# A decoder in one kernel: norm's root ahead of weight splits, embeddings transposed ahead of the bias, a tile's softmax sums transposed behind its own probabilities

## The reference

```python
x = x + recurrent(layernorm(x))                 # conv, gates, a linear scan, GELU gate, output product
x = x + aft(layernorm(x) + ctx, pos_bias, ...)  # keys, values, exp(pos_bias) band, two layernorms, an MLP
for l in range(2):                              # attention over windows of 128 tokens, then an MLP
    q, k, v = split(shift(x) @ wqkv[l]); q, k = rotary(l2norm(q) * qs), rotary(l2norm(k) * ks)
    p = exp(q @ k.T + mask)                     # 8 heads of 64; a tile of 128 queries sees two tiles of keys
    x = x + ((p @ v) / p.sum(-1)) @ wo[l]
    x = x + mlp(layernorm(shift(x)))
```

## Time and profile before

| | |
|---|---|
| time, median of 3 runs | 1028.35 us (1028.14 to 1028.93) |
| the profiled execution: time, span | 1023.85 us, 1022.0 us |
| busy: PE, DVE | 949.0 us (93%), 664.5 us (65%) |
| busy: ACT, POOL | 511.1 us (50%), 414.3 us (41%) |
| mean TensorE clock granted | 0.987 of full speed |

### The profile page before, as it was taken

One profiled execution on the slowest core, in us unless ns is written; L12 is line 12 of the kernel. 1 busy time (PEld: TensorE's weight loads), 2 busy tenths in 40 slices (PEclk: granted clock), 3 DMA queues, 4 the chain that ended last, 5 costly groups with the idle time before them and its releaser, 6 DMA issues.

```text
span 1022.0 us, 17391 instructions
## 1 busy us (share of the span) xinstructions
PE 949.0 (93%) x5656; PEld 766.2 (75%) x5656; DVE 664.5 (65%) x1686; ACT 511.1 (50%) x1217; POOL 414.3 (41%) x416
## 2 busy tenths in 40 slices
PE   5889969999999997999999889999999999979998
PEld 4668855767676875888888777888787878768887
DVE  6879576357574577667666545667766676745653
ACT  4577731403122234666666664444766666664443
POOL 4333523112012247766767410004766666621110
PEclk9899979999999998999999999999999999999999
DMA  6202013000000000000000020000000000100101
GB/s 248 73 1 62 21 42 108 1 0 1 0 0 1 1 22 0 2 23 0 21 0 28 16 93 23 4 4 23 1 2 22 0 21 0 35 15 17 32 24 45
DMA packets 15236, 26.32 MB, mean 26 GB/s; under 512 B 1162, under 2 KB 11776, under 8 KB 14416
## 3 DMA queue, kind: packets, MB, share of 16 engines
q1 hardware_dynamic: 15184, 25.68, 7.7%
HBM read 20.53 MB, written 2.10 MB: 22 GB/s over the span
## 4 chain that ended last, share of the span: by engine, by line
PE 74%; DVE 9%; ACT 6%; issue 4%; POOL 4%; SPq 2%; DMA 1%; DVEq 0%; ACTq 0%; POOLq 0%
PE bank L1540 31%; PE bank L1874 6%; PE bank L1687 5%; PE bank L1829 5%; PE bank L1735 5%; PE bank L1839 4%; PE bank L1853 4%; ACT probs L1406 2%; PE bank L1816 2%; PE bank L1864 2%; SPq L342 1%; PE bank L1698 1%; PE bank L1947 1%; PE bank L1808 1%; POOL scanned L410 1%
## 5 line engine op out<-in xcount | busy, mean ns | idle before, releaser
L1406 ACT ACTIVATE probs<-bank,row_min 128x256 f32<-128x256 f32 (+1 forms) x256 | 111.6, 463 | 122.6 <-DVE row_min L998 122.6
L542 POOL TENSOR_TENSOR norms<-norms,minus_half 128x16 f32<-128x16 f32 x32 | 93.6, 2924 | 2.7
L998 DVE CUSTOM_DVE_ANT_0 bank<-bank,mask 128x256 f32<-128x256 f32 (+1 forms) x256 | 90.8, 429 | 5.7 <-PE bank L1829 5.6
L1540 PE MATMUL bank<-wqkv_hi,x_hi 128*128 128x512 f32 x192 | 82.5, 430 | 1.8 <-DVE rot L974 1.1
L1540 PE MATMUL bank<-wqkv_lo,x_hi 128*128 128x512 f32 x192 | 76.3, 398 | 0.0
L1540 PE MATMUL bank<-wqkv_hi,x_lo 128*128 128x512 f32 x192 | 75.9, 395 | 0.0
L1135 DVE SCALAR_TENSOR_TENSOR hidden<-bank,lcols,hidden 128x512 f32<-128x512 f32 (+1 forms) x48 | 36.0, 750 | 50.9 <-PE bank L1540 28.2
L1839 PE MATMUL bank<-ident,probs 128*128 128x128 f32 x448 | 61.5, 279 | 3.7 <-ACT probs L1406 3.7
L524 POOL TENSOR_TENSOR q_tok<-rot 128x512 f32<-128x512 f32 x32 | 41.3, 1290 | 57.7 <-DVE rot L974 57.7
L1540 PE MATMUL bank<-t_hi,wm_hi 128*128 128x512 f32 x160 | 63.6, 397 | 0.0
L1540 PE MATMUL bank<-t_lo,wm_hi 128*128 128x512 f32 x160 | 63.5, 397 | 0.0
(11 more groups left out here) (240 smaller groups left out, 2642.5 us busy)
## 6 DMA issues: line engine op xcount, KB each, us to landing
w_stage<-in_wm_l_dram SPq DMA_DIRECT2D x8, 534.0 KB, 3.7
w_stage<-in_wqkv_dram SPq DMA_DIRECT2D x2, 1536.0 KB, 7.9
out_dram<-stream SPq DMA_DIRECT2D x8, 256.0 KB, 2.4
emb<-in_ctx_dram SPq DMA_DIRECT2D x1, 1536.0 KB, 6.7
inner<-in_w_gate_dram SPq DMA_DIRECT2D x1, 1152.0 KB, 10.1
stream<-in_x_dram SPq DMA_DIRECT2D x2, 512.0 KB, 5.6
stream<-in_x_dram SPq DMA_DIRECT2D x1, 1024.0 KB, 12.5
ew<-in_pos_bias_dram SPq DMA_DIRECT2D x1, 1024.0 KB, 11.3
```

The source lines that it names most:

```text
L542: pool.tensor_tensor(norms[:, 2, :], norms[:, 1, :], minus_half[:, :], ALU.pow).then_inc(c_rn, 1)
L998: dve.tensor_tensor_reduce(logits, logits, mask[:, 2 * P - nk:2 * P], 1.0, FAR, ALU.add, ALU.min, row_min[:, w % 2, 2 * i + e:2 * i + e + ...
L1406: act.activation(probs[:, i, e, 0:nk], logits, ACT.Exp, bias=row_min[:, w % 2, h:h + 1], scale=-1.0, accum_out=row_sum[:, w % 2, h:h + 1]) ...
L1540: ins = pe.matmul(out, stationary, moving, start=(first and i == 0), stop=(last and i == len(terms) - 1))
```

## The change

Four places change; no computation is added or removed.

1. First stage: POOL splits the first of the three gate weight pieces ahead of `rstd_of(1)` and not behind it; DVE makes `m4sp` between the statistics of batch 1 and their use; ACT makes `gelu_gate(0)` ahead of `transposed_out(1)`.
2. Second stage: `rstd_of(NB)` stands ahead of the seven weight splits on POOL.
3. `transpose_emb(0)` stands ahead of `bias_by_key(0)` on PE, and its copies in the same place on ACT.
4. Attention: `transpose_sums(n)` stands in window n, behind the last transpose of its probabilities, and writes bank 3; ACT's copy stands behind the copy of the last transposed probabilities. `weigh_values` waits for that copy, since it writes bank 3 next, and `transpose_k` for the residual of n - 2.

```diff
@@ POOL
             rstd_of(0)
-            rstd_of(1)
-
             pool.wait_ge(wg_in, 16)
             for k in range(KR):
+                if k == 1:
+                    rstd_of(1)
...
+            rstd_of(NB)
             pool.wait_ge(wx_in, 64)
...
             pool.wait_ge(aft_in, 48)
-            rstd_of(NB)
             keep_emb(0)
@@ DVE
             dve.wait_ge(a_tp, 2)
-            norm(1, 1)
+            norm_stats(1, 1)
             dve.wait_ge(col_in, 16)
-            conv_taps(0, 0)
-            conv_taps(0, 1)
-            low_part(1, a_tp_out, a_tp_lo)
-            conv_low(0, 0)
-            conv_taps(0, 2)
-            conv_low(0, 1)
             dve.tensor_scalar(fb_tmp[:, 2, :], cols[:, C_FB:C_FB + KR], 0.0, None, ALU.max).then_inc(fb_vec, 1)
...
             dve.tensor_scalar(m4sp[:, :], fb_tmp[:, 2, :], -4.0, None, ALU.mult).then_inc(fb_vec, 1)
+            norm_apply(1, 1, False)
+            conv_taps(0, 0)
+            conv_taps(0, 1)
+            low_part(1, a_tp_out, a_tp_lo)
+            conv_low(0, 0)
+            conv_taps(0, 2)
+            conv_low(0, 1)
             conv_low(0, 2)
@@ ACT
             taps(0)
+            gelu_gate(0)
             transposed_out(1)
-            gelu_gate(0)
...
+            transposed_emb(0)
             bias_transposed(0)
             bias_transposed(1)
-            transposed_emb(0)
...
                 act.wait_ge(c_ot_out, n)
-                act.activation(rsum_t[:, :], bank[2][:, :], ACT.Copy).then_inc(c_rt_out, 1)
+                act.activation(rsum_t[:, :], bank[3][:, :], ACT.Copy).then_inc(c_rt_out, 1)
...
                 exps(n, w, 1)
-                if prev:
-                    sums_transposed(n - 1)
...
                 probs_transposed(n, w, KI - 1)
+                sums_transposed(n)
                 if two:
                     values(n + 2, (w + 2) % TT)
...
-                sums_transposed(n0 + NT - 1)
@@ PE
+            transpose_emb(0)
             bias_by_key(0)
             bias_by_key(1)
-            transpose_emb(0)
...
                 pe.wait_ge(c_v, n + 1)
-                pe.wait_ge(c_ot_out, n)
+                pe.wait_ge(c_rt_out, n + 1)
...
                 pe.wait_ge(c_rb, n + 1)
-                if not (isinstance(n, int) and n == 0):
-                    pe.wait_ge(c_res, n)
+                pe.wait_ge(c_ot_out, n)
                 for i in range(KI):
-                    ins = pe.transpose(bank[2][:, i * P:(i + 1) * P],
+                    ins = pe.transpose(bank[3][:, i * P:(i + 1) * P],
...
                 if keyed:
                     pe.wait_ge(c_qt, n + 3)
+                else:
+                    pe.wait_ge(c_res, n)
...
                 score_pairs(n, w)
                 if prev:
-                    transpose_sums(n - 1)
                     weigh_values(n - 1, (w - 1) % TT)
...
-                    transpose_k(n + 1, (w + 1) % 2, [(c_rt_out, n)] if prev else [])
+                    transpose_k(n + 1, (w + 1) % 2, [(c_res, n - 1)] if prev else [])
...
                 transpose_probs(n, w, KI - 1)
+                transpose_sums(n)
                 if two:
                     qkv(n + 2, (w + 2) % TT, 2)
...
-                transpose_sums(n0 + NT - 1)
                 weigh_values(n0 + NT - 1, TT - 1)
```

## The result

| | before | changed |
|---|---|---|
| time, median | 1028.24 us (1027.26 to 1028.93, 4 runs) | 1012.3 us (1011.3 to 1013.42, 4 runs) |
| the profiled execution: time, span | 1023.85, 1022.0 us | 1013.18, 1011.4 us |
| its mean granted TensorE clock | 0.987 | 0.985 |

The ratio is 0.9845, with a 95% interval of 0.9823 to 0.9868: 15.9 us faster.

What follows compares the result with a forecast made beforehand. PE, busy 93% of the span, bounds the kernel, with holes where it waits for DVE. Terms 9.5 + 0.8 + 5.2 = 15.5 us off 1023.85 give 1008.35, plus 4.5 to the median: 1012.9 us, range 1007.5 to 1018.5.

Steps and rivals of the forecast that it cites:

- The second stage: Root ahead of POOL's weight splits, embeddings' transposes ahead of the bias: `project` starts 9.5 us earlier.
- The sign of error that I had named: Forecast is wrong if PE idles ahead of the sums' transposes or `project` waits for POOL's low parts beyond 135.
- The rival of strict turns: POOL and DVE alternate strictly: second stage gives 7.9 us, 11.7 us in all, 1016.7 us; chance 0.2.
- The first stage: Root of batch 1 1.0 us later, taps 1.9 us shorter: PE starts 0.8 us earlier.
- The attention: Sums' transposes moved behind the probabilities: 2.6 us off a layer, 5.2 us for two.
- The ordinary window: PE-bound attention windows, n = 2 to 12 without w = 1: 0.18 us off each, 1.6 us in nine.
- the new change from scores to weighing: PE's shape change in attention windows: bounds nothing to 0.37 us, taken as 0.19.
- n = 14: Attention tile waiting on DVE's keys: 1.0 us of idling goes, less 0.5 for the sums, 0.5 us off.
- The last tile: End of an attention layer: ACT's copies end earlier, output product at 599.25 instead of 600.06, 0.8 us off.
- The sums' wait: Rival: PE waits for the sums in each of some 26 attention windows, 1031 us at 0.7 us each; chance 0.04.
- The gain of the second stage: Rival had it given back, the residual waiting for something else: only 6.0 us left, 1022.4 us; chance 0.04.
- the free change: Rival: attention's new shape change free, clock up at the bias, DVE held little: 19.7 us off, 1008.7 us; chance 0.17.

Runs made afterwards that it cites:

- the first experiment: The changed kernel timed once more without any edit (also called the repeat): 1010.92 us, 0.9837 of the kernel before.
- early splits and a later `keep_emb(0)`: Changed kernel with the ten weight splits moved to where POOL idles and `keep_emb(0)` behind DVE's low part of the embeddings: 1008.61 us.
- the root put back: Changed kernel with POOL making the first stage's root of batch 1 ahead of all gate splits again: 1013.93 us.
- last experiment: Changed kernel with the weighing of tile n - 1 behind two thirds of the product of n + 2 on PE: 1049.13 us.
- the attention's part alone: Kernel before with only the change's attention hunks: 1021.62 us, ratio 0.9938.
- the three groups: Experiments timed beside the kernel before, each group sharing a chip; medians of before 1027.98, 1027.63 and 1029.88 us.

## Why the prediction held, and where it didn't

The time was in the range, 0.6 us from the forecast. By its steps:

**The second stage.** Forecast 9.5 us, measured 10.05 to `project`; the low clock in the profiled execution then took back 1.5 us of it there, and in the execution of the first experiment nothing. DVE's pieces came as placed: `normed` 2.57 (2.4), the gated inputs 3.81 (3.9), the wait 1.41. My bias at half its slow time (0.97) measured 1.06; of the 10.05 us, 0.9 are the bias at the full clock. What I had under-estimated is how the splits suffer: 10.3 us instead of 7.8. The low parts that `project` waits for ended at 135.47, as late as DVE's own (135.49) and PE's bias (135.50). My "at 130.8 if nothing holds them" left out that they are held, and by luck this cost nothing. The sign of error that I had named, `project` waiting for low parts beyond 135, came by the letter; but this execution's statistics ended 2.2 us later than before's, so counted as in before they ended at 133.3. The rival of strict turns, 12.5 us of work one after the other, gives 125.26 + 12.5 = 137.8 for the last split; it came at 135.5, between this and no hold. The operation that takes one input from PSUM was not held: the residual took 1.27 us for two beside the low splits, as in the earlier trace rows. This is what the Trainium skill says (GPSIMD Engine Reference, Key points: contention with VectorE's instructions that have two SBUF inputs or a two-port mode), and with early splits and a later `keep_emb(0)` each held operation came down to its free time, 1.38, 1.22 and 1.89 us. Here the page warned rightly of the hold, and the root's earlier place was worth far more.

**The first stage.** Forecast 0.8 us, measured 0.64 in the profiled execution and 0.9 between the earlier trace rows and the repeat (28.82). The root was 1.3 us later instead of 1.0, because POOL began with the gate weights at 13.29; taps 4.78 us against my 4.9. The experiment with the root put back shows the mechanism.

**The attention.** Forecast 2.6 us a layer. The terms, with what they measured:

- The ordinary window: 0.18 forecast, 0.13, 0.15 and 0.16 by its place, 1.3 us instead of 1.6 in nine. The mis-sized part is the new change from scores to weighing: I took 0.19 of 0.37, it is 0.22, since the scores' piece takes 1.93 us whether sums, weighing, or the product (last experiment) stand behind it. My reading that the change into the scores is free was wrong too. In the changed trace the scores start two by two. Counted from start to start, 0.31 us lie between the last output product and the first pair of scores and 0.32 between the first pair and the second, where both kinds follow each other at 0.216: some 0.2 us for this change. By the same count scores to weighing costs 0.14 us, weighing to product 0.2, and product to the keys' transposes nothing (0.231, as between products). The Trainium skill's rule of a drain at each change of tiling mode (TensorEngine Tiling (Array Packing), Tiling Modes) agrees in direction.
- w = 1: 0.04 forecast and measured. n = 0: 0.44 forecast and measured in layer 1; in layer 0 it is 0.4 in the changed trace and 0.5 in the repeat (15.61 us).
- n = 14: forecast 0.5 us off. Where neither has a low clock, 12.80 (layer 1 of before) became 11.89 (layer 0 of the changed kernel), 0.9 us. Where both have one, in layer 0, 14.02 became 12.97 in the repeat, 1.1 us. But PE waits long for the keys there (2.54 us, before 3.06), and a low stretch of the clock can follow: in layer 1 it did in each trace of the changed order and in none of the old one, and 0.2 us was lost. This term failed as I put it, for it has more than one value.
- The last tile: forecast 0.8, measured 0.6. `rsum_t` was copied from 586.27 on, the output product began at 589.91, 14.65 us behind the tile's scores instead of 15.26.

Added up from the first score of n = 0 to the last tile's output product, the repeat is 2.65 us shorter than before in layer 0 and 1.46 in layer 1: 4.1 us against the forecast 5.2. The missing 1.1 us are n = 14 of layer 1 (0.7), the ordinary windows (0.6) and the ends of the layers (0.4), less 0.6 that n = 14 of layer 0 gave beyond its 0.5.

**The sum.** 10.0 + 0.9 + 4.1 = 15.0 us. That this is so near the forecast 15.5 is in part luck: the second stage gave 0.5 us more than forecast and the attention 1.1 less. In the profiled pair it is 10.7: of the difference, 2.85 us are the low stretch at 60:80, 1.5 the one in `project`, 1.0 the one at 900:910, less 1.1 because n = 14 of layer 0 had none: 4.25 of 4.3 us. The medians give 15.9 and, in the repeat, 16.7 us; what they give beyond 15.0 lies inside their intervals. A part of it may be that a hole in PE's work can cost more than its length: in the trace with the attention's part alone, which has the old hole, the clock is low from 135.1 to 148.7, and `project` to the first score takes 1.6 us longer than in before. Before's profiled execution, at 1023.85, was below all of its 37 runs of the three groups (1024.0 to 1032.48), the changed kernel's near its slowest (1008.85 to 1013.42). The forecast survived this since it added the gap of 4.5 us between execution and median to both. That step was an assumption that I had not named: it holds only if the changed kernel's low stretches are as many as before's.

**The rivals.** The sums' wait didn't come: no idle time stands ahead of L1862 in the changed kernel's two traces. The gain of the second stage was kept. Strict turns and the free change were both wrong in their main term, and the sum lay between them; the free change was the second one's premise, and the starts above speak against it.

What stays open is why the low stretches at 60:80 and 900:910 are there in some executions and not in others.

## What to carry to other kernels

Before an operation of a few columns that another engine waits for, ask what is queued ahead of it: one root of 1 us behind ten splits cost 6.3 us alone and 10 with the transposes moved along. Then look for the work that is displaced: it was better put where its engine idled anyway than right behind the root. And compare medians or distances between two events in the same trace, not the ends of two profiled executions, when PE's clock has low stretches.

## What the hardware did that I had not expected

POOL's own splits lengthen beside DVE: a high part 0.96 us (3.83 for four) instead of 0.60, a low part 1.54 instead of 1.24, while in the first stage the gate splits of 768 columns kept 0.85 to 0.89 and 1.84 to 1.86 us beside `normed` and the same `normed` took 5.66 us. So which of the two is held more differed between the two places; the runs don't show on what it depends.

One low stretch in busy work cost 1.0 to 2.9 us, and executions of one program on one chip differed by up to 8.2 us, in step with the mean granted clock (0.987 to 0.978). PE had idled ahead of those that I followed: 1.72 us ahead of the bias and `project`, 8.67 in the earlier trace rows; but 2.54 us at n = 14 of layer 0 of the changed kernel's first profiled execution brought no low stretch, nor did 3.06 us at n = 14 of layer 1 in any of the four traces with the old order, so idle time alone doesn't tell.
